# Router product and flip of h2 as one product, with the fourth block's result in the second bank of mix

## The chip, the cores and the metric

The kernel runs on one core of a Trainium2 chip. The metric is the device time in microseconds of one execution; of the kernel before, three runs were timed. One further execution was recorded by the profiler; all rows below come from that one.

## What is computed

A transformer block with adaptive layer norm on x of shape 16 x 512 x 128 (16 batches, 512 tokens, 128 channels), all in fp32:

```
h = layernorm(x) * (1 + ca) + sa
x = x + ga * attention(h)                  # Q = K = V = h @ Wq + bq, one head, softmax
h = layernorm(x) * (1 + cb) + sb           # "h2" in the kernel
route = sigmoid(h @ Wr + br)               # 8 experts
e = argmax(route);  p = max(route)
x = x + gb * p * (gelu(h @ W1[e]) @ W2[e]) # W1 128x512, W2 512x128 per expert
```

sa, ca, ga, sb, cb, gb are rows made from a conditioning input, one per batch. The change touches the line `h @ Wr` and the way in which h2 gets back from its flipped form into rows of tokens.

## The kernel before, in words

**Two phases.** The attention phase handles the 16 batches in slots k = -2 to 15 (`attention_slots`). The second phase handles the expert layer over tiles of up to 256 tokens that are sorted by expert (39 tiles, `ffn_slots`). Between them stand some hand-written steps for batches 14 and 15, whose routing is not done when the last slot ends. Each engine (TensorE `pe`, ScalarE `act`, VectorE `dve`, GpSimd `pool`, the DMA queue `sp`) has its own list of work, written out by hand, and takes it strictly in that order; semaphores join the lists. There is no planner: the functions named `slot(k)` are the order.

**One attention slot k on TensorE** (line 630). Five batches are in the works at once: `before2` (k-2), `before` (k-1), `now` (k), `after` and `after2`. A batch has J = 4 blocks of 128 tokens. The slot's list is: second score product of `now` (score, lines 500 to 502, three fp32r matmuls of 512 columns), flip of the first block's probabilities (L512, four transposes), fourth mix of `before` (L525, eight matmuls), projection of `after` (L479), third score product of `now`, **router of `before2`** (L545), flip of the second block's probabilities, first mix of `now`, fourth score product of `now`, flip of v (L487), **flip of h2 of `before2`** (L555), flip of the third block's probabilities, second mix of `now`, first score product of `after`, fourth flip, places of `before2` (L569 to L575), third mix, and two flips of normalised rows (L469, and L537 for h2 of `before`). In the last slot (k = 15) the first tiles of the second phase are woven in (flip_rows, L587; up, L608 to L610).

**One attention slot on VectorE** (line 1158): maximum of the second scores (`find_max`, L937), third residual of `before` (`residual`, L956) with its statistics (L963), statistics of x for `after2`, maximum of the third scores of `now`, **fourth residual of `before`**, **bias addition of `before2`** (`add_bias`, L989), statistics, split of q (L919), maximum of the fourth scores, choice of the expert of `before2` in six small steps (L1004 to L1021) between other work, first maximum of `after`, slot numbers of `before2` (L1032 to L1044). In slots 13 and 14 chains of tiny instructions that plan the first tiles (`early_plan`) come on top, and in slot 15 VectorE fills the first tile's weights (`fill_slots(0)`, L1073 and L1078) ahead of the maximum of the third scores.

**ScalarE** does the exponentials (L747), the copies of flipped probabilities (L755), scale and shift of h2 into `h2_t` (`router_input`, L763), the exponential for the router (`logit_exp`, L778), the copy of the flipped-back h2 into the payload rows (`ffn_input`, L771) and in the second phase the gelu (L804).

**The path of h2 before the change.** `flip_xn2` puts the normalised rows, flipped, into PSUM bank `side[0]`; ScalarE makes `h2_t` from it (128 channels on partitions, 4 x 128 tokens). `router` multiplies each 128x128 block of `h2_t` (the stationary operand) with Wr (128 x 8, the moving operand) into 4 x 8 columns of `side[0]`. VectorE adds the bias from there. Only when it has read them (`logit_ready`) does `flip_h2` flip the same four blocks back into rows of tokens, over all 512 columns of `side[0]`; `ffn_input` copies them into the payload, and `places` waits for that copy (`h2_ready`) before it uses `side[0]` again. `mix(b, j)` writes the first 128 columns of bank `mixed[j % 2]`, and `residual(b, j)` reads them; the second phase's `down(t)` writes the first 256 columns of `mixed[t % 2]` and `finish(t)` (L1098) reads them.

**The hand-written steps between the phases.** TensorE: fourth mix of batch 15, router(14), down(0), flip_h2(14), up(1), places(14), flip_rows(2), down(1) (L625), flip_xn2(15), up(2), router(15), flip_rows(3), down(2), flip_h2(15), up(3), places(15), and so on. ScalarE: logit_exp(14), ffn_input(14), gelu(1) and so on, where an exponential and a gelu each need their own table, loaded by an instruction of its own.

## Time and profile before

| | |
|---|---|
| median of three runs | 354.69 us (354.61 to 355.04) |
| the profiled execution's own time | 354.34 us |
| span of its profile | 352.6 us |
| TensorE busy | 325.0 us, 92% of the span |
| VectorE busy | 278.9 us, 79% |
| ScalarE busy | 223.5 us, 63% |
| GpSimd busy | 193.1 us, 55% |
| mean granted clock of TensorE | 0.986 of 2.4 GHz |

The span runs from the first to the last instruction of the profile; the execution's own time has 1.74 us around it. PE is TensorE's matmul, PEld its weight load, which overlaps with matmuls; DVE is VectorE, ACT ScalarE, POOL GpSimd. Instructions of one engine overlap by some 0.06 to 0.1 us at their ends, so that the pace of a sequence is read from start to start, not from durations. An fp32 matmul is issued as two weight loads and two matmuls; a transpose as one of each.

### The profile page before, as it was taken

The numbers are of one execution on the slowest core, as the hardware profiler recorded it, in microseconds if no ns is written. First come the engines' busy times: TensorE is split into PE (matmuls) and PEld (weight loads), VectorE is DVE, ScalarE is ACT, GpSimd is POOL, SyncE is SP. The second block draws the span as 40 slices with busy tenths as digits, with TensorE's granted clock in tenths as the row PEclk, the third lists the DMA queues.
The fourth block names the chain that finished last, engine by engine and source line by source line (L and its number), as shares of the span: only waits on it lengthen the run. The fifth ranks groups of instructions, "written<-read, shape, count | busy, mean of one in ns | idle before, by whom it ended". The sixth has DMA issues, their size and how long they took to land.

```text
span 352.6 us, 8419 instructions
## 1 busy us (share of the span) xinstructions
PE 325.0 (92%) x2578; PEld 299.6 (85%) x2578; DVE 278.9 (79%) x1114; ACT 223.5 (63%) x477; POOL 193.1 (55%) x224
## 2 busy tenths in 40 slices
PE   2799999999999999999989898899999999999960
PEld 2388788889888988898878798899999999999960
DVE  5378898898889888988997896899897777877730
ACT  2589987888788878887866585654445454434320
POOL 5016467545754575457525445877566556565661
PEclk9999999999999999999999999999999999999995
DMA  3394124337653666943536612664989554454300
GB/s 113 116 256 104 44 68 131 100 112 121 146 105 104 123 128 188 249 138 111 105 91 224 231 50 87 186 205 134 289 259 307 166 171 120 127 139 125 93 21 4
DMA packets 34493, 49.27 MB, mean 140 GB/s; under 512 B 4320, under 2 KB 26115, under 8 KB 34448
## 3 DMA queue, kind: packets, MB, share of 16 engines
q1 hardware_dynamic: 27504, 31.74, 37.0%
q0 software_dynamic: 6368, 16.92, 12.9%
q8 instruction: 21, 0.34, 0.4%
q14 instruction: 24, 0.20, 0.2%
q10 hardware_dynamic: 576, 0.07, 0.1%
HBM read 28.21 MB, written 20.96 MB: 139 GB/s over the span
## 4 chain that ended last, share of the span: by engine, by line
PE 70%; DVE 13%; ACT 6%; issue 5%; DVEq 2%; DMA 1%; POOL 1%; POOLq 0%; SPq 0%; ACTq 0%
PE mixed L625 14%; PE mixed L525 12%; PE flipped L512 6%; PE side L479 4%; PE scores L502 3%; PE scores L500 3%; PE scores L501 3%; PE side L545 3%; PE side L469 2%; PE scores L609 2%; PE scores L610 2%; PE scores L608 2%; PE side L537 2%; PE side L487 2%; PE flipped L609 2%
## 5 line engine op out<-in xcount | busy, mean ns | idle before, releaser
L1406 POOL DMA_INDIRECT sorted_rows<-payload,slots x64 | 63.9, 998 | 79.8 <-DVE slots L1044 64.9
L1433 POOL DMA_INDIRECT out_dram<-y_out,tokens x71 | 74.9, 1055 | 42.4 <-DVE y_out L1105 25.8
L625 PE MATMUL mixed<-down_slot,hidden 128*128 128x128 f32 x568 | 70.1, 276 | 2.5 <-ACT hidden L804 2.5
L625 PEld LDWEIGHTS mixed<-down_slot,hidden 128*128 128x128 f32 x568 | 66.5, 192 | 3.0 <-ACT hidden L804 3.0
L525 PE MATMUL mixed<-v_sb,probs_t 128*128 128x128 f32 x512 | 69.0, 278 | 0.0
L747 ACT ACTIVATE probs<-scores,row_max 128x512 f32<-128x512 f32 x64 | 44.0, 687 | 35.1 <-DVE row_max L937 33.4
L525 PEld LDWEIGHTS mixed<-v_sb,probs_t 128*128 128x128 f32 x512 | 62.2, 192 | 0.2
L937 DVE TENSOR_REDUCE row_max<-scores 128x1 f32<-128x512 f32 x64 | 44.1, 688 | 19.0 <-PE scores L502 19.0
L789 ACT ACTIVATE f_hi<-side 128x256 fp32r<-128x256 f32 (+1 forms) x39 | 14.3, 366 | 42.8 <-PE side L587 42.8
L512 PE MATMUL flipped<-ident,probs 128*128 128x128 f32 x256 | 39.1, 275 | 0.4 <-ACT probs L747 0.3
L755 ACT ACTIVATE probs_t<-flipped 128x512 f32<-128x512 f32 x64 | 37.9, 594 | 0.0
L512 PEld LDWEIGHTS flipped<-ident,probs 128*128 128x128 f32 x256 | 31.1, 145 | 5.9 <-ACT probs L747 1.9
L500 PE MATMUL scores<-q_hi,q_lo 128*128 128x512 f32 x64 | 35.7, 557 | 0.0
L1073 DVE CAST up_slot<-w_parts 128x1024 fp32r x39 | 28.0, 719 | 3.2 <-issue 1.4
L708 ACT ACTIVATE xn<-x_tile,offset,rstd 128x128 f32<-128x128 f32 x64 | 26.2, 491 | 5.2 <-POOL offset L1379 5.2
L1376 POOL TENSOR_TENSOR rstd<-var,neg_half 128x4 f32<-128x4 f32 x16 | 19.9, 1243 | 15.7 <-DVE var L875 15.4
L804 ACT ACTIVATE hidden<-flipped 128x512 f32<-128x512 f32 x38 | 22.5, 597 | 7.9 <-PE flipped L610 6.0
L1078 DVE COPY down_slot<-w_sb 128x512 f32 x39 | 17.5, 448 | 11.4 <-PE mixed L625 11.4
L502 PE MATMUL scores<-q_hi 128*128 128x512 f32 x64 | 25.5, 398 | 0.0
L501 PE MATMUL scores<-q_lo,q_hi 128*128 128x512 f32 x64 | 25.3, 396 | 0.0
L1098 DVE SCALAR_TENSOR_TENSOR gated<-mixed,rows 128x128 f32<-128x128 f32 x71 | 21.6, 341 | 3.0 <-PE mixed L625 3.0
L608 PE MATMUL scores<-f_lo,up_slot 128*128 128x256 f32 (+1 forms) x80 | 23.5, 294 | 0.0
(187 smaller groups left out, 768.7 us busy)
## 6 DMA issues: line engine op xcount, KB each, us to landing
rows<-sorted_rows SPq DMA_DIRECT2D x32, 388.0 KB, 3.7
x_tile<-in_L_attn_inputs_dram SPq DMA_DIRECT2D x16, 256.0 KB, 3.2
payload<-stored_gates SPq DMA_DIRECT2D x16, 256.0 KB, 9.3
sorted_rows<-pad_rows SPq DMA_DIRECT2D x9, 388.0 KB, 4.6
w_parts<-in_L_ffn_W_dram SPq DMA_DIRECT2D x1, 2048.0 KB, 8.8
rows<-sorted_rows SPq DMA_DIRECT2D x7, 194.0 KB, 2.6
out_dram<-y_out,tokens POOLq DMA_INDIRECT x71
gate<-stored_gates SPq DMA_DIRECT2D x16, 64.0 KB, 5.8
```

Of the source, the lines that this page charges most:

```text
L500: nc.tensor.matmul(o, q_lo[:, b.p, mine], q_hi[:, b.p, :], start=True, stop=False)
L501: nc.tensor.matmul(o, q_hi[:, b.p, mine], q_lo[:, b.p, :], start=False, stop=False)
L502: nc.tensor.matmul(o, q_hi[:, b.p, mine], q_hi[:, b.p, :], start=False, stop=True).then_inc(scores_ready, 1)
L512: last = nc.tensor.transpose(flipped[j % 2][:, k * P:(k + 1) * P], probs[:, j % 2, k * P:(k + 1) * P], ident[:])
L525: last = nc.tensor.matmul(mixed[j % 2][:, 0:H], probs_t[:, j % 2, k * P:(k + 1) * P], v_sb[:, b.p, k, :], start=(k == 0), stop=(k == J - 1))
L608: nc.tensor.matmul(o, hi, f_lo[:, t % 2, 0:width], start=True, stop=False)
L625: last = nc.tensor.matmul(mixed[t % 2][:, u * H:(u + 1) * H], hidden[:, t % 2, f, u * P:(u + 1) * P], down_slot[:, t % 3, f, :], start=(f ...
L747: nc.scalar.activation(probs[:, j % 2, :], scores[j % 2][:], ACT.Exp, bias=row_max[:, c:c + 1], accum_out=den[:, c:c + 1]).then_inc(exp_do ...
L755: nc.scalar.activation(probs_t[:, j % 2, :], flipped[j % 2][:], ACT.Copy).then_inc(probs_t_ready, 1)
L937: nc.vector.tensor_reduce(row_max[:, c:c + 1], scores[j % 2][:], AX_X, ALU.max, negate=True).then_inc(max_found, 1)
L1406: nc.gpsimd.indirect_dma_start(rows_dram, bass.IndirectOffsetOnAxis(ap=slots[:, c:c + 1], axis=0), payload[:, b.q, j, :], None).then_inc(s ...
L1433: nc.gpsimd.indirect_dma_start(out_rows, bass.IndirectOffsetOnAxis(ap=tokens[:, t % RING, u:u + 1], axis=0), y_out[:, t % RING, u, :], Non ...
```

## The change

- `ident` and `wr_sb` become two parts of one buffer `ident_wr` of 128 + 8 columns.
- `router` now multiplies each block of `h2_t` with this 136-column moving operand: the first 128 columns of the result are the block flipped back, the last 8 the logits. Blocks 0 to 2 lie in `side[0]` at a step of 136 columns; block 3, for which that bank has no room, in columns 256 to 391 of `mixed[1]`. `flip_h2` is gone.
- Before the fourth product TensorE waits until the fourth residual of the batch before has been read out of `mixed[1]` (`x1_ready`), and for the last batch until tile 1 of the second phase has (`gated_ready`).
- Before the second mix of a slot, which writes `mixed[1]`, TensorE waits for the bias addition and for ScalarE's copy of block 3.
- ScalarE copies block 3 with an instruction of its own (`ffn_input_part`, right behind `logit_exp`), and blocks 0 to 2 where it copied all four.
- VectorE adds the bias in two instructions, block 3 first. Between the phases `finish(1)` moves ahead of `add_bias(15)`.

```diff
-        ident = sb("ident", [P, P])
+        ident_wr = sb("ident_wr", [P, P + E])
+        ident = ident_wr[:, 0:P]
...
-        wr_sb = sb("wr_sb", [P, E])
+        wr_sb = ident_wr[:, P:P + E]
...
+        def h2_bank(j):
+            if j == J - 1:
+                return mixed[1][:, 2 * H:3 * H + E]
+            return side[0][:, j * (H + E):(j + 1) * (H + E)]
...
                 wait(pe, x1_ready, J * b.n + j - 1)
+                if j == 1:
+                    wait(pe, logit_ready, b.n - 1)
+                    wait(pe, h2_part_ready, b.n - 1)
                 for k in range(J):
                     last = nc.tensor.matmul(mixed[j % 2][:, 0:H], probs_t[:, j % 2, k * P:(k + 1) * P],
...
                 pe.wait_ge(h2t_ready, b.n + 1)
                 for j in range(J):
-                    last = nc.tensor.matmul(side[0][:, j * E:(j + 1) * E], h2_t[:, j * P:(j + 1) * P],
-                                            wr_sb[:], start=True, stop=True)
-                last.then_inc(logits_ready, 1)
-
-            def flip_h2(b):
-                if not real(b):
-                    return
-
-                pe.wait_ge(logit_ready, b.n + 1)
-                for j in range(J):
-                    last = nc.tensor.transpose(side[0][:, j * P:(j + 1) * P], h2_t[:, j * P:(j + 1) * P],
-                                               ident[:])
-                last.then_inc(h2_flipped, 1)
+                    if j == J - 1:
+                        pe.wait_ge(x1_ready, min(J * (b.n + 2), J * B))
+                        if b.n == B - 1:
+                            pe.wait_ge(gated_ready, 4)
+                    last = nc.tensor.matmul(h2_bank(j), h2_t[:, j * P:(j + 1) * P], ident_wr[:],
+                                            start=True, stop=True)
+                last.then_inc(h2_routed, 1)
...
                 flip_v(after)
-                flip_h2(before2)
                 if ending:
...
             down(0)
-            flip_h2(last_but_one)
             up(1)
...
             down(2)
-            flip_h2(last_one)
             up(3)
...
                 act.wait_ge(xn2_flipped, b.n + 1)
-                wait(act, h2_flipped, b.n)
+                wait(act, h2_routed, b.n)
...
+            def ffn_input_part(b):
+                if not real(b):
+                    return
+                act.wait_ge(logit_ready, b.n + 1)
+                wait(act, scattered[b.q], 16 * J * b.r)
+                nc.scalar.activation(payload[:, b.q, J - 1, 0:H], h2_bank(J - 1)[:, 0:H], ACT.Copy
+                                     ).then_inc(h2_part_ready, 1)
+
             def ffn_input(b):
                 if not real(b):
                     return
-                act.wait_ge(h2_flipped, b.n + 1)
-                wait(act, scattered[b.q], 16 * J * b.r)
-                nc.scalar.activation(payload[:, b.q, :, 0:H], side[0][:].rearrange("p (j h) -> p j h", j=J),
-                                     ACT.Copy).then_inc(h2_ready, 1)
+                nc.scalar.activation(payload[:, b.q, 0:J - 1, 0:H], side[0][:, 0:(J - 1) * (H + E)].rearrange(
+                    "p (j h) -> p j h", j=J - 1)[:, :, 0:H], ACT.Copy).then_inc(h2_ready, 1)
...
                 logit_exp(before2)
+                ffn_input_part(before2)
...
-                dve.wait_ge(logits_ready, b.n + 1)
-                nc.vector.tensor_tensor(logit[:].rearrange("p (j e) -> p j e", e=E),
-                                        side[0][:, 0:J * E].rearrange("p (j e) -> p j e", e=E),
-                                        br_sb[:].unsqueeze(1).to_broadcast([P, J, E]), ALU.add
+                dve.wait_ge(h2_routed, b.n + 1)
+                nc.vector.tensor_tensor(logit[:, (J - 1) * E:J * E], h2_bank(J - 1)[:, H:H + E], br_sb[:], ALU.add)
+                nc.vector.tensor_tensor(logit[:, 0:(J - 1) * E].rearrange("p (j e) -> p j e", e=E),
+                                        side[0][:, 0:(J - 1) * (H + E)].rearrange("p (j h) -> p j h", j=J - 1)[:, :, H:H + E],
+                                        br_sb[:].unsqueeze(1).to_broadcast([P, J - 1, E]), ALU.add
                                         ).then_inc(logit_ready, 1)
...
             fill_slots(3)
+            finish(1)
             add_bias(last_one)
-            finish(1)
             split_lo(3)
```

## Rows read from the trace of the kernel before

**Rows 1.** The page: busy us (share of the span), instructions, of all engines.

```profile
PE 325.0 (92%) x2578; PEld 299.6 (85%) x2578; DVE 278.9 (79%) x1114; ACT 223.5 (63%) x477; POOL 193.1 (55%) x224
```

**Rows 2.** Three windows: PE, PEld, DVE, ACT, POOL busy, TensorE's clock, DMA share, GB/s.

```profile
0.00:20.00 20.00, 11.10 (x38) 7.25 (x39) 9.63 (x42) 8.32 (x17) 4.86 (x21) 1.00 0.45 146
100.00:140.00 40.00, 40.00 (x308) 35.95 (x307) 35.40 (x165) 33.20 (x76) 23.33 (x28) 1.00 0.57 132
180.00:220.00 40.00, 36.15 (x295) 32.90 (x295) 31.90 (x141) 26.84 (x55) 18.19 (x20) 1.00 0.39 133
```

**Rows 3.** Timeline of TensorE in one ordinary slot: start, duration (us), line, matmuls.

```profile
161.44 0.39 PE L502 MATMUL scores<-q_hi 128*128 128x512 f32 x1
161.67 0.95 PE L545 MATMUL side<-wr_sb,h_t 128*128 128x8 f32 x8
162.48 0.63 PE L512 MATMUL flipped<-ident,probs 128*128 128x128 f32 x4
162.95 1.06 PE L525 MATMUL mixed<-v_sb,probs_t 128*128 128x128 f32 x8
163.76 0.47 PE L500 MATMUL scores<-q_hi,q_lo 128*128 128x512 f32 x1
...
164.97 0.60 PE L555 MATMUL side<-ident,h_t 128*128 128x128 f32 x4
165.40 0.60 PE L512 MATMUL flipped<-ident,probs 128*128 128x128 f32 x4
```

**Rows 4.** Timeline of VectorE in the same slot; in brackets idle time, releaser.

```profile
161.87 0.69 DVE L937 TENSOR_REDUCE row_max<-scores 128x1 f32<-128x512 f32 x1 [0.28 <-PE scores L502]
162.48 0.34 DVE L956 SCALAR_TENSOR_TENSOR payload<-mixed,den_inv,x_tile 128x128 f32<-128x128 f32 x1
162.74 0.18 DVE L989 TENSOR_TENSOR logit<-side,br_sb 128x32 f32<-128x32 f32 x1
162.86 0.29 DVE L963 BATCH_NORM_STATS2 stats<-payload 128x6 f32<-128x128 f32 x1
...
164.73 0.69 DVE L937 TENSOR_REDUCE row_max<-scores 128x1 f32<-128x512 f32 x1 [0.57 <-PE scores L502]
```

**Rows 5.** Timeline of ScalarE in the same slot: the fourth exponential.

```profile
165.46 0.69 ACT L747 ACTIVATE probs<-scores,row_max 128x512 f32<-128x512 f32 x1 [1.47 <-DVE row_max L937]
```

**Rows 6.** Waits of TensorE, whole span: us in total, times, longest.

```profile
PE side L537 <- DVE batch_count L1035: 2.0, 2, 1.4
```

**Rows 7.** Timeline, last slot and after it: where TensorE starts behind a wait.

```profile
202.14 0.17 DVE L989 TENSOR_TENSOR logit<-side,br_sb 128x32 f32<-128x32 f32 x1
...
202.37 0.66 PE L555 MATMUL side<-ident,h_t 128*128 128x128 f32 x4
...
209.23 1.06 PE L545 MATMUL side<-wr_sb,h_t 128*128 128x8 f32 x8
...
210.15 2.03 PE L625 MATMUL mixed<-down_slot,hidden 128*128 128x128 f32 x16
```

**Rows 8.** Timeline behind the attention phase, ScalarE and TensorE.

```profile
212.65 0.60 ACT L771 ACTIVATE payload<-side 128x512 f32<-128x512 f32 x1 [1.87 <-PE side L555]
...
213.27 1.28 ACT L804 ACT_TABLE_LOAD   x1
...
215.70 2.05 PE L625 MATMUL mixed<-down_slot,hidden 128*128 128x128 f32 x16 [1.26 <-ACT hidden L804]
```

**Rows 9.** Timeline of the last slot, TensorE and VectorE.

```profile
200.09 0.63 PE L512 MATMUL flipped<-ident,probs 128*128 128x128 f32 x4
...
201.88 0.34 DVE L956 SCALAR_TENSOR_TENSOR payload<-mixed,den_inv,x_tile 128x128 f32<-128x128 f32 x1
201.91 0.40 PE L502 MATMUL scores<-q_hi 128*128 128x512 f32 x1
...
202.88 0.68 DVE L937 TENSOR_REDUCE row_max<-scores 128x1 f32<-128x512 f32 x1
```

More of the change, by code:

```diff
@@ L260, in adaln_block @@
         h2t_ready = sem("h2t_ready")
-        logits_ready = sem("logits_ready")
+        h2_routed = sem("h2_routed")
         logit_ready = sem("logit_ready")
@@ L271, in adaln_block @@
         ids_ready = sem("ids_ready")
-        h2_flipped = sem("h2_flipped")
+        h2_part_ready = sem("h2_part_ready")
         h2_ready = sem("h2_ready")
@@ L844, in _ @@
             logit_exp(last_but_one)
+            ffn_input_part(last_but_one)
             ffn_input(last_but_one)
@@ L851, in _ @@
             logit_exp(last_one)
+            ffn_input_part(last_one)
             ffn_input(last_one)
```

## The prediction

> **What bounds the kernel now.** I read the page first: TensorE is busy 92% of the span, VectorE 79% [rows 1]. That is a mean over stages, so next came the windows. In the middle of the attention phase TensorE is busy for all of its 40 us while VectorE and ScalarE have room; in the last slots of that phase it stands idle for 3.85 us of 40 [rows 2]. Then the timeline of one slot, engine by engine. On TensorE groups follow each other without a gap [rows 3], so in such a slot every nanosecond that TensorE issues less is a nanosecond won, and every wait that is put into its queue is a nanosecond lost. VectorE waits for the third score product before its row maximum, 0.28 us, and again 0.57 us before the next one [rows 4]; ScalarE stands idle 1.47 us before the fourth exponential [rows 5]. The last view is the list of waits: where TensorE waits longest inside the attention phase, it is in two slots for VectorE [rows 6].
>
> **What is removed.** The flip of h2, four transposes. From its start to the next group's start is 165.40 - 164.97 = 0.43 us [rows 3]. It goes once per batch, 16 times: 6.9 us if TensorE is what counts everywhere.
>
> **What the wider product costs.** The router's four fp32 products are issued as eight weight loads and eight matmuls. With 8 moving columns they take 162.48 - 161.67 = 0.81 us; the eight matmuls of a mix, with 128 moving columns, take 163.76 - 162.95 = 0.81 us too [rows 3]. So 8 or 128 columns cost the same 0.10 us per matmul and 136 will cost at most 136/128 of that, 0.107 us: 0.05 us for all eight. The Trainium skill (TensorE: Matmul & The Clock Gate, section "Wait — 56ns, not 53.3ns?") puts a matmul of very few columns at a floor near 25 ns and a wide one at N/2.4 + 2.5 ns, which is 59 ns at 136; by that the widening would be an estimated 0.03 us for each matmul and 0.27 us per batch, and most of the saving would go; the rows show equal times at 8 and 128 columns, so the measurement decides.
>
> **What is added: the wait before the fourth product.** The fourth result lies in the second bank of mix, so TensorE waits there until VectorE has made the fourth residual of the batch before, which reads that bank. In VectorE's queue that residual stands behind the row maximum of the third score product, and that product is the group that TensorE has just finished. So the wait is a round trip that starts when TensorE arrives:
> - scores end at 161.44 + 0.39 = 161.83 [rows 3], row maximum starts 161.87, residual starts 162.48 and ends 162.82 [rows 4];
> - a wait of TensorE on VectorE ends 0.06 us after the releasing instruction (VectorE 202.14 + 0.17 = 202.31, TensorE 202.37) [rows 7]: 162.88;
> - the first three products need 6 x 0.10 = 0.61 us from 161.67 and are through at 162.28, so TensorE stands 0.60 us;
> - a start from standstill is dearer: the router's eight pairs that start right behind a wait take 210.15 - 209.23 = 0.92 us [rows 7], against 0.81. I take 0.11;
> - the fourth product's two pairs: 0.21 us.
> The next group starts at 163.20, not 162.48: +0.72. With the flip gone (-0.43) the slot is **longer by 0.29 us**. Bounds: without the dearer start and at 0.10 us a pair, +0.17; if instead the full weight load ahead of the first matmul and a later signal are paid, +0.40.
>
> The Trainium skill (PSUM — Partial Sum Buffer, section "PSUM bank collisions raise a hardware error") says that two engines may not touch one bank at once even at different columns, and to guard by bank: by that rule this wait can't be left out though the columns are disjoint. No run here shows a collision; it changes no number above.
>
> **What queues behind.** TensorE: flip and mix of the next probabilities, the fourth score product, all later by 0.72, by 0.29 after the place of the old flip. VectorE: the bias addition waits for the fourth product, which ends about 0.42 us after its start (1.06 us for eight less six of 0.107 [rows 7]), at 163.30; two small additions take about 0.12 us each, as the one does from 162.74 to 162.86 [rows 4]. What follows is late by about 0.7 us, but the next row maximum had 0.57 us of idle time in front of it and its product comes 0.72 later, so this stays covered. If the cover fails, each slot pays up to 0.1 more. ScalarE's extra copy costs at most the whole copy's 0.60 [rows 8] and lies in the 1.47 us of [rows 5]. TensorE's other new wait, before the second mix, asks for that copy. The additions are through near 163.6; one copy of probabilities, one small exponential and this copy, at most 1.4 us together, bring it to 165.0, and the flip ahead of that mix starts only at 165.40 + 0.29 = 165.69 [rows 3]: nothing. No DMA is added or moved; scatters on GpSimd wait for slot numbers, which shift with everything else.
>
> **The sum, slot by slot.** The router product runs in 14 attention slots.
> - 11 ordinary ones: 11 x 0.29 = +3.2.
> - Two slots in which VectorE is the bound, since it also makes the early plan; TensorE waits there for VectorE, up to 1.4 us [rows 6]. The removed flip brings nothing, and the round trip holds VectorE at its bias addition: +0.72 each, +1.4.
> - The last slot. VectorE first fills the expert weights, so the residual starts at 201.88 and ends 202.22 [rows 9]. TensorE's fourth product can start at 202.28, the next group at 202.60, not 200.09: +2.5. The fourth score product starts 201.91 + 2.51 = 204.42 and ends 204.82; its row maximum, which ran at 202.88 [rows 9], starts at 204.86: **+1.98**. The exponentials, the last flip, the choice of expert and the first up product hang on it one after another.
> - Behind the attention phase: ScalarE's copy no longer waits for the flip (1.87 us idle before it), so the table load behind it and the gelu of tile 1 come earlier, and with them the down product that waited 1.26 us [rows 8]. But VectorE's chain, over the normalised rows that GpSimd's power gives, then decides, which leaves 0.5; the wait of the last batch's fourth product for tile 1's gating takes that back; the same at tile 3 leaves about 0.2. I take **-0.2**; bounds -1.4 (the whole wait) and +0.5.
> Sum: 3.2 + 1.4 + 2.0 - 0.2 = +6.4 us.
>
> The profiled execution took 354.34 us (span 352.6 and 1.74 around it); the median of the runs is 354.69, 0.35 above it. On the median: 354.69 + 6.4 = **361.1 us**.
>
> **Rivals.**
> 1. The wait doesn't hold TensorE: the residual is there when TensorE reaches the fourth product. Then only the saving counts: 16 x (0.43 - 0.05) = -6.1 us, 348.6. It decides from the point at which the residual ends before 162.28, and in the rows it ends 0.54 later in every ordinary slot, because the row maximum in front of it waits for TensorE itself. Chance 0.05.
> 2. A draw: TensorE starts again without loss (+0.17 for 11 slots, 1.9), the last slot's and the plan slots' delays are taken up by the idle time around them (up to 3 of 3.4), and the down product gains its whole 1.26. Sum near +1, 355.6; each part would have to fall the kind way. Chance 0.07 for anything from here to 357.
> 3. VectorE's cover fails: held by the fourth product, it comes late to its maximum in every slot, the fourth exponential and flip follow. Price: the 0.40 bound and 0.1 more for 14 slots, +3 on the sum, 364. For it speaks that 0.57 is less than 0.7; against it that the product is late by the same 0.72. Chance 0.13.
> 4. The standstill of some 2.4 us in the last slot lowers TensorE's granted clock. In the first 20 us TensorE is busy for 11 us only and the clock stays at 1.00, 2.4 GHz [rows 2], so I hold it unlikely; it would cost what the next few us of work lose at the lower level, 1 to 2 us, inside the range. Chance 0.03.
> My own case has the remaining 0.72.
>
> **How the numbers follow.** The bounds: 11 x 0.17 + 2 x 0.5 + 1.0 - 1.4 = +2.5, and 11 x 0.40 + 2 x 0.9 + 2.3 + 0.5 = +9.0. Both ends need every term at its bound at once, so I cut the low one only a little (+2.8, 357.5) and the high one nowhere near rival 3's 364 (364.0). Within 0.2% (0.7 us, about what a measurement of this kernel can tell from no change) lies a corner of rival 2: 0.02. Faster: rival 1 and the far end of rival 2: 0.06. Slower: 0.92.
>
> **What would show it.** Right: in ordinary slots TensorE stands 0.6 us inside the router line, waiting for the residual line; the distance from one batch's router line to the next grows by about 0.3 us; the bias additions wait for the router line; the last slot shows a stand of over 2 us. The eight wide matmuls of the batch after the attention phase take 0.9 to 1.0 us. Wrong: no idle time on TensorE before the fourth product (rival 1); row maxima of the fourth product without any idle time before them (rival 3); a distance between router lines that shrinks by 0.4 us.

## The result, and the profile after

| | before | after |
|---|---|---|
| median (six runs each) | 354.87 us (354.59 to 355.69) | 364.68 us (363.48 to 365.65) |
| the profiled execution's own time | 354.34 us | 364.71 us |
| span | 352.6 us | 363.0 us |

The change makes the kernel slower: ratio 1.0273, 95% interval 1.0256 to 1.0290. The forecast was 361.1 us with a range to 364.0: the direction was right, the size was 3.6 us short, and the result lies outside the range.

The page of the kernel after, busy us (share of the span) and instructions, against [rows 1]:

```profile
PE 328.7 (91%) x2514; PEld 296.7 (82%) x2514; DVE 281.2 (77%) x1130; ACT 226.2 (62%) x493; POOL 190.5 (52%) x224
```

TensorE has 64 instructions fewer (the flips) and 3.7 us more busy time. Where the 10.4 us of span came from shows in the distances from one batch's router line to the next, batch by batch (start of L545 before, of L558 after, read from the timelines):

| stretch | before | after | difference |
|---|---|---|---|
| start to the first router line | 43.28 | 43.39 | +0.11 |
| first distance | 12.60 | 12.66 | +0.06 |
| ten ordinary slots, together | 117.56 | 123.54 | +5.98 (0.60 each) |
| the two slots of the early plan | 13.51, 12.33 | 14.16, 12.99 | +0.65, +0.66 |
| the last slot | 9.95 | 12.98 | +3.03 |
| between the phases | 10.22 | 9.88 | -0.34 |
| router line of batch 15 to the end | 133.15 | 133.40 | +0.25 |

The sum is +10.4. The ten ordinary distances are 11.75 to 11.77 before; after, eight are 12.31 to 12.36, one is 12.39 and one 12.47. So a slot of the steady kind costs 0.58. The first distance hardly grows, although the wait is there too: in it TensorE waits for VectorE's `mask` in both kernels, 0.28 us before and 0.17 after, and both times reaches the line behind that wait about 6.75 us after the router line.

Timeline of TensorE in one ordinary slot of the kernel after (the one of [rows 3], now 5.53 us later):

```profile
166.97 0.39 PE L508 MATMUL scores<-q_hi 128*128 128x512 f32 x1
167.20 0.86 PE L558 MATMUL side<-ident_wr,h_t 128*128 128x136 f32 x6
168.40 0.50 PE L558 MATMUL mixed<-ident_wr,h_t 128*128 128x136 f32 x2 [0.35 <-DVE payload L965]
168.74 0.60 PE L518 MATMUL flipped<-ident_wr,probs 128*128 128x128 f32 x4
...
170.53 0.39 PE L508 MATMUL scores<-q_hi 128*128 128x512 f32 x1
```

VectorE in that slot, against [rows 4], in the same view:

```profile
167.40 0.69 DVE L946 TENSOR_REDUCE row_max<-scores 128x1 f32<-128x512 f32 x1 [0.27 <-PE scores L508]
168.00 0.34 DVE L965 SCALAR_TENSOR_TENSOR payload<-mixed,den_inv,x_tile 128x128 f32<-128x128 f32 x1
168.94 0.17 DVE L998 TENSOR_TENSOR logit<-mixed,br_sb 128x8 f32<-128x8 f32 x1 [0.59 <-PE mixed L558]
...
170.96 0.69 DVE L946 TENSOR_REDUCE row_max<-scores 128x1 f32<-128x512 f32 x1 [0.56 <-PE scores L508]
```

ScalarE, against [rows 5]:

```profile
171.69 0.69 ACT L747 ACTIVATE probs<-scores,row_max 128x512 f32<-128x512 f32 x1 [1.43 <-DVE row_max L946]
```

The router line to the next line is 168.74 - 167.20 = 1.54 us, against 0.81: +0.73. It is the round trip that was forecast: TensorE stands behind its six matmuls until the residual is through (168.00 + 0.34 = 168.34, start 168.40). The idle time in front of the fourth maximum is as before, 0.56 us. So up to here the slot went as forecast. The list of waits of TensorE over the whole span, against [rows 6]:

```profile
PE mixed L558 <- DVE payload L965: 7.1, 14, 2.2
```

Fourteen waits for the residual, one per attention slot with a router line. (The view counts idle time from the modelled end of the sixth matmul; the six take 0.69 from start to start, as in the kernel with the residual first below, so the stand is 168.40 - 167.89 = 0.51.)

What the forecast didn't have shows only at the end of the slot. TensorE, ScalarE and VectorE there, in three cuts of the timeline of the kernel after:

```profile
161.49 1.14 PE L534 MATMUL mixed<-v_sb,probs_t 128*128 128x128 f32 x8
162.58 0.66 PE L475 MATMUL side<-ident_wr,xn 128*128 128x128 f32 x4
163.17 0.63 PE L546 MATMUL side<-ident_wr,xn 128*128 128x128 f32 x4
163.55 0.47 PE L506 MATMUL scores<-q_hi,q_lo 128*128 128x512 f32 x1
```

```profile
160.88 1.64 ACT L708 ACTIVATE xn<-x_tile,offset,rstd 128x128 f32<-128x128 f32 x4
```

```profile
158.63 0.69 DVE L946 TENSOR_REDUCE row_max<-scores 128x1 f32<-128x512 f32 x1 [0.55 <-PE scores L508]
...
162.83 0.19 DVE L1042 TENSOR_TENSOR place<-side,region 128x32 f32<-128x32 f32 x1
```

The same lines of the kernel before, in an ordinary slot:

```profile
132.74 1.14 PE L525 MATMUL mixed<-v_sb,probs_t 128*128 128x128 f32 x8
133.72 0.60 PE L469 MATMUL side<-ident,xn 128*128 128x128 f32 x4
134.15 0.60 PE L537 MATMUL side<-ident,xn 128*128 128x128 f32 x4
134.51 0.48 PE L500 MATMUL scores<-q_hi,q_lo 128*128 128x512 f32 x1
```

```profile
129.47 0.69 DVE L937 TENSOR_REDUCE row_max<-scores 128x1 f32<-128x512 f32 x1 [0.57 <-PE scores L502]
...
133.70 0.18 DVE L1032 TENSOR_TENSOR place<-side,region 128x32 f32<-128x32 f32 x1
```

After the change the flip of the normalised rows (L475) starts 0.06 us behind the end of ScalarE's four normalisations (162.52), and the flip behind it (L546) 0.15 us behind the end of VectorE's `place` (163.02), whose source bank it overwrites. Before, `place` ended at 133.88 and the flip came 0.27 later, in TensorE's own time. From the third mix to the first score product the kernel after takes 2.06 us, the one before 1.77 (134.51 - 132.74): 0.29 of the flip's 0.43 are lost here.

That makes the slot a **loop of two engines**: TensorE from that flip to the end of the fourth score product, then VectorE from the fourth row maximum to `place`, then the flip again. After: 163.17 to 170.92 is 7.75, the hand-over 0.04, VectorE's list 158.63 to 163.02 is 4.39, the hand-over back 0.15; sum 12.33, which is the distance measured. Before: 7.03 (L537 at 157.66, L502 ending at 164.69), 0.04 and 4.41; with the hand-over back of the kernel after, 0.15, they make 11.63, while TensorE's own list makes 11.75. The loop lay only 0.12 us under TensorE's list, though no wait showed it. The flip of h2 lies outside the loop (it comes behind the fourth score product), the new wait lies inside.

The last slot in the kernel after, TensorE's timeline, against [rows 9]:

```profile
206.74 0.86 PE L558 MATMUL side<-ident_wr,h_t 128*128 128x136 f32 x6
209.76 0.50 PE L558 MATMUL mixed<-ident_wr,h_t 128*128 128x136 f32 x2 [2.16 <-DVE payload L965]
210.10 0.60 PE L518 MATMUL flipped<-ident_wr,probs 128*128 128x128 f32 x4
...
212.23 0.63 PE L507 MATMUL scores<-q_lo,q_hi 128*128 128x512 f32 x1
212.66 0.63 PE L508 MATMUL scores<-q_hi 128*128 128x512 f32 x1
```

and the windows of that stretch (PE, PEld, DVE, ACT, POOL busy, TensorE's clock, DMA share, GB/s), against [rows 2]:

```profile
210.00:211.00 1.00, 1.00 (x11) 1.00 (x11) 0.64 (x4) 0.26 (x1) 0.00 (x0) 1.00 0.53 199
211.00:212.00 1.00, 1.00 (x7) 1.00 (x6) 0.17 (x1) 0.62 (x3) 0.73 (x1) 0.51 0.00 0
...
214.00:215.00 1.00, 1.00 (x9) 1.00 (x8) 1.00 (x9) 0.95 (x3) 0.00 (x0) 0.79 0.00 0
```

TensorE stands for 2.3 us (six products through at 206.74 + 0.69 = 207.43, next start 209.76), and from about 211 to 214.4 its clock is granted at 0.50, 1.2 GHz. From the flip at 210.10 to the third score matmul at 212.66 are 2.56 us; the same steps take 170.53 - 168.74 = 1.79 in the ordinary slot: 0.77 lost to the clock. That matmul itself then takes 0.63 instead of 0.39, another 0.24.

### The profile page after: what moved, and what is told of

It is laid out like the page before. It is cut to its first block and busy times, and to the rows that moved or that the text cites. A ratio compares the mean times of both kernels' runs of the same rounds, so it can differ in the third digit from the quotient of the medians.

```text
span 363.0 us, 8338 instructions
## 1 busy us (share of the span) xinstructions
PE 328.7 (91%) x2514; PEld 296.7 (82%) x2514; DVE 281.2 (77%) x1130; ACT 226.2 (62%) x493; POOL 190.5 (52%) x224
## 5 line engine op out<-in xcount | busy, mean ns | idle before, releaser
L518 PE MATMUL flipped<-ident_wr,probs 128*128 128x128 f32 x256 | 39.2, 276 | 0.4 <-ACT probs L747 0.3
L518 PEld LDWEIGHTS flipped<-ident_wr,probs 128*128 128x128 f32 x256 | 31.7, 143 | 5.6 <-ACT probs L747 1.5
L1083 DVE CAST up_slot<-w_parts 128x1024 fp32r x39 | 27.2, 698 | 3.0 <-issue 1.4
L1088 DVE COPY down_slot<-w_sb 128x512 f32 x39 | 19.2, 493 | 13.0 <-PE mixed L628 13.0
L1386 POOL TENSOR_TENSOR rstd<-var,neg_half 128x4 f32<-128x4 f32 x16 | 17.7, 1105 | 16.1 <-DVE var L884 15.8
```

The costliest lines, as they stand in the source:

```text
L518: last = nc.tensor.transpose(flipped[j % 2][:, k * P:(k + 1) * P], probs[:, j % 2, k * P:(k + 1) * P], ident[:])
L1083: nc.vector.tensor_copy(up_slot[:, t % 2, :, :].rearrange("p s f -> p (s f)"), w1_parts[:].rearrange("p e s f -> p (e s f)")[:, bass.ds(w ...
```

## The experiments

In the expectations "theory P" is the prediction's reckoning, in which the removed flip counts in full, "theory L" is the loop above, and "theory C" an earlier form of it. On two chips the kernel before itself has a median of 370 to 374 us, and in most ordinary slots of the traces taken there ScalarE stands still before a copy, for up to 1.5 us, without a cause in the trace ("disturbed" below). Every ratio is against the runs of before on the same chip. A slot without such a stand isn't a clean measure there either: in the kernel without the flip it has 11.78 and 11.81 us, against 11.64 for the same slot on a quiet chip.

**The wait alone.** The kernel before, with the wait and nothing else; the flip stays.

```diff
                 for j in range(J):
+                    if j == J - 1:
+                        pe.wait_ge(x1_ready, min(J * (b.n + 2), J * B))
                     last = nc.tensor.matmul(side[0][:, j * E:(j + 1) * E], h2_t[:, j * P:(j + 1) * P],
```

> The kernel before with one thing added: TensorE waits before the fourth router product (still 8 columns, still in the first side bank) until the fourth residual of the batch before is made. The flip of h2 stays. Theory C (the wait costs 0.73 us in every slot; the flip that is removed in the changed kernel brings back only about 0.14 of its 0.43 us, since behind the fourth score product the lists of VectorE and ScalarE are only some 0.2 us shorter than TensorE's; and the stand of over 2 us in the last slot drops TensorE's clock to 1.2 GHz for about 3 us, 1.0 us more): distance between router lines 12.47 us, 11 x 0.72 + 2 x 0.7 + 2.0 + 1.0 = +12.3, about 367 us, with a window of clock 0.5 behind the last slot's wait. Theory P (the prediction's sum: the flip is worth its whole 0.43 and the clock stays): the same distance 12.47, no lower clock, +11.3, 366. Both fall if the distance stays near 11.75 to 12.0.

Measured: 381.34 us against 373.22 there, ratio 1.0213 (1.0138 to 1.0288). All ten ordinary distances are 12.40 to 12.42 (although ScalarE stands still there too): the wait alone costs a slot 0.65 us, more than the whole change (0.58). The wait carries the loss, and all the rest of the change brings 0.07. In the last slot TensorE stands until 210.25, and its granted clock is 0.50 from 211.6 to 215.0, as theory C had it. The total grew by 8.1 us and not by the 11 or 12 of either theory; on this chip that can't be taken apart.

**The flip alone.** The kernel before without the flip of h2; its result, the rows of h2 in the payload, is then missing.

```diff
-                pe.wait_ge(logit_ready, b.n + 1)
-                for j in range(J):
-                    last = nc.tensor.transpose(side[0][:, j * P:(j + 1) * P], h2_t[:, j * P:(j + 1) * P],
-                                               ident[:])
-                last.then_inc(h2_flipped, 1)
+                return
...
-                wait(act, h2_flipped, b.n)
+                wait(act, logits_ready, b.n)
...
-                act.wait_ge(h2_flipped, b.n + 1)
+                act.wait_ge(logit_ready, b.n + 1)
```

> The kernel before without the four transposes of h2; everything else stays, the router with 8 columns and no new wait. It leaves out the flip back of h2, so the rows of h2 that go to the experts hold other numbers; routing is the same. Theory P: every ordinary slot is 0.43 us shorter, distance 11.32, and about 0.3 from the copy behind the attention phase: 354.7 - 4.7 - 0.3 = 349.7 us. Theory C: TensorE waits at the end of each slot instead, for the normalised x of ScalarE and for VectorE's slot numbers; distance 11.6 to 11.65, 353 us.

> The same kernel as in the run without the flip of h2 (the four transposes are left out, the rows of h2 for the experts hold other numbers), on another call, since ScalarE and VectorE stood for up to 1.5 us in many slots of that run for nothing in the kernel. Theory L (the ordinary slot is a loop of two engines: TensorE from the last flip of a slot to the fourth score product, 7.0 us, then VectorE's list from that product's row maximum to the slot numbers, 4.4 us, together 11.5 with their signals, against 11.75 of TensorE's own work; so 0.43 us less TensorE work can't bring more than 0.2): distance 11.55 to 11.65, 352.5 to 353.5 us if the kernel before takes 354.7. Theory P (the flip counts in full): 11.32, 349.7 us.

> The kernel before without the flip of h2 a third time (the four transposes left out, other numbers in the rows of h2), since the first two were on a chip on which the kernel before takes 373 to 374 us. Theory L (a loop of TensorE and VectorE's list behind the fourth score product, 11.5 us long with its signals): distance between router lines 11.55 to 11.65 and 352.5 to 353.5 us where the kernel before takes 354.7. Theory P (TensorE's work is the bound and the flip counts in full): 11.32 and 349.7 us. Theory S (ScalarE's 1.4 us stands before the copy of the second flipped probabilities belong to the other chip): none of them here; if they are here too they belong to the kernel.

Measured: 0.9962 (0.9917 to 1.0007) and 0.9839 (0.9681 to 0.9997) on a disturbed chip, which doesn't settle a few tenths per cent; on a chip with 354.67 for before it is 353.11, ratio 0.9950 (0.9932 to 0.9969), 1.6 us. Nine of the ten distances are 11.61 to 11.67 and one is 11.73, mean 11.66: leaving out 0.43 us of TensorE's work shortens the slot by 0.10, as theory L had it (11.55 to 11.65); theory P had 11.32. The end of the slot in that kernel, TensorE and VectorE:

```profile
167.53 1.14 PE L525 MATMUL mixed<-v_sb,probs_t 128*128 128x128 f32 x8
168.69 0.66 PE L469 MATMUL side<-ident,xn 128*128 128x128 f32 x4
169.24 0.63 PE L537 MATMUL side<-ident,xn 128*128 128x128 f32 x4
169.63 0.47 PE L500 MATMUL scores<-q_hi,q_lo 128*128 128x512 f32 x1
```

```profile
168.93 0.17 DVE L1028 TENSOR_TENSOR place<-side,region 128x32 f32<-128x32 f32 x1
```

Mix to score product takes 2.10 us (1.77 before), and the flip starts 0.14 behind the end of `place`, as in the kernel after. The 0.12 of the loop's slack is what can be had, and 0.10 was.

**One bank.** All four wide products in `side[0]`, the fourth first; block 3 overlaps block 2 by 32 columns, so its result is partly overwritten. No wait, no second bank.

```diff
-                return mixed[1][:, 2 * H:3 * H + E]
+                return side[0][:, 512 - H - E:512]
...
-                if j == 1:
-                    wait(pe, logit_ready, b.n - 1)
-                    wait(pe, h2_part_ready, b.n - 1)
...
-                for j in range(J):
-                    if j == J - 1:
-                        pe.wait_ge(x1_ready, min(J * (b.n + 2), J * B))
-                        if b.n == B - 1:
-                            pe.wait_ge(gated_ready, 4)
+                for j in (J - 1, 0, 1, 2):
```

> The changed kernel with all four wide products in the first side bank, the fourth computed first and 32 of its columns overwritten by the third (so that 32 of 128 columns of h2 are wrong in every fourth block; routing is right); the wait for the residual and both waits before the second mix are gone, everything else as changed. It takes away the second bank and nothing else. Theory P: no stand in the router, distance 11.37, 354.7 - 11 x 0.38 - 0.2 = 350.3 us. Theory C: distance 11.6, waits of 0.2 to 0.3 us in all before the two flips at the slot's end as in the changed kernel, clock 1.00 in the last slot, 352.5 to 353.5 us. Both: the second bank costs over 10 us.

> The same kernel as in the run with all four wide products in the first side bank (32 of 128 columns of h2 wrong in every fourth block), repeated for the same reason. Theory L: distance 11.60 to 11.65, 353 us; theory P: 11.37, 350.3 us.

Measured: ratio 0.9928 (0.9878 to 0.9978), then 0.9867 (0.9665 to 1.0069), distance in the one slot of each trace that has no stand of ScalarE 11.83 and 11.82, in most others 11.80 to 11.95. Against the 12.33 of the kernel after the loss is gone, and the 11.37 of theory P doesn't show. Whether a saving of a tenth or two is in it this chip can't tell, since the kernel without the flip has 11.78 and 11.81 in that slot here. The ratios below 1 aren't explained by these slots.

**The residual first.** The kernel after with one line moved on VectorE: the fourth residual goes ahead of the maximum of the third scores, so that it no longer stands behind the product that TensorE has just made.

```diff
+                residual(before, 3)
                 if planning:
                     early_plan(0)
...
                 find_max(now, 2)
...
-                residual(before, 3)
```

> The changed kernel with VectorE's fourth residual of the batch before moved ahead of the row maximum of the third scores (in slots 13 and 15 also ahead of the plan and of the filling of weights). The result stays right. If the wait is the round trip over the row maximum, the stand in the router disappears (0.00 instead of 0.35 to 0.60 us) and with it the one of 2.2 us in the last slot and the lower clock. Theory P: distance 11.37, 350.5 us. Theory C: distance 11.6, 353 us, a little under the kernel before. A rival to both: the row maximum comes 0.1 to 0.3 later because the residual lies in front of it and the exponentials follow, distance 11.7 to 11.9, 355 us.

> The same kernel as in the run with the fourth residual ahead of the row maximum, repeated for the same reason. Theory L: no stand in the router, distance 11.60 to 11.65, 353 us; theory P: 11.37, 350.5 us.

> The changed kernel with the fourth residual ahead of the third row maximum, again. Theory L: no stand in the router, distance 11.60 to 11.65, 352.5 to 353.5 us, a little faster than the kernel before. Theory P: 11.37, 350.5 us. If the changed kernel's loss were not the wait: over 360 us.

Measured: 0.9858 (0.9741 to 0.9975) and 0.9934 (0.9891 to 0.9977) on the disturbed chip; on a chip with 354.67 for before 354.92, ratio 1.0008 (0.9995 to 1.0021). TensorE's timeline in a slot of the last of these:

```profile
162.81 0.86 PE L558 MATMUL side<-ident_wr,h_t 128*128 128x136 f32 x6
163.50 0.40 PE L558 MATMUL mixed<-ident_wr,h_t 128*128 128x136 f32 x2
163.73 0.60 PE L518 MATMUL flipped<-ident_wr,probs 128*128 128x128 f32 x4
```

The residual (162.63 + 0.34 = 162.97) is through before the fourth product needs it. The router line takes 0.92 us, the clock in the last slot stays at 1.00, and eight of the ten distances are 11.74 to 11.78, the others 11.81 and 11.86. Theory L had 11.60 to 11.65 here and missed: its loop has the router line with 8 columns. TensorE's part of it runs from the flip to the end of the fourth score product, and the router line lies inside:

```profile
158.75 0.63 PE L546 MATMUL side<-ident_wr,xn 128*128 128x128 f32 x4
...
165.53 0.39 PE L508 MATMUL scores<-q_hi 128*128 128x512 f32 x1
```

That is 7.17 us, against 7.03 before; with 0.04, 4.41 and 0.15 the loop is 11.77, which is the distance measured. The 0.11 of the wider product uses up the 0.12 that the removed flip could have brought.

One moved line gives back all 9.8 us: the wait with what hangs on it is the whole loss, and what is left of the change, flip removed and product widened, is worth nothing as the kernel stands.

**What the loop holds back.** To the kernel with the residual first, a second move: the choice's first two steps ahead of the fourth row maximum, which shortens VectorE's list inside the loop.

```diff
-                find_max(now, 3)
                 choose(before2, 0)
                 invert_den(now, 0)
                 choose(before2, 1)
+                find_max(now, 3)
                 residual(now, 0)
```

> The changed kernel with the fourth residual first and, besides, three small VectorE instructions (the first two of the choice of expert and the reciprocal of the sums) moved from behind the fourth row maximum to ahead of it, into idle time. The result stays right. Theory L: VectorE's list behind the fourth score product is 0.3 us shorter, so the loop is 11.3 and TensorE's own work of 11.37 counts: distance 11.35 to 11.45, 11 x 0.35 plus the parts of the later slots, about 349.5 us, faster than both kernels. Theory P: the three moves change nothing against the run with the residual first, since TensorE is the bound there already. A rival: the exponential of the logits is not ready when VectorE gets to them, VectorE waits in front of the fourth row maximum and the distance grows to 11.7 or more.

> As before this, with the first two steps of the choice and the reciprocal also ahead of the fourth row maximum, again. Theory L: VectorE's list behind the fourth score product 0.3 us shorter, distance 11.35 to 11.45, about 350 us. On the other chip VectorE waited 0.86 us for the exponential of the logits and the distance was 12.4; if that belongs to the kernel, it is 12.4 here too and 361 us.

Measured: on the disturbed chip 1.0121 (0.9963 to 1.0279), nine of the ten distances 12.40 to 12.57. VectorE waits there for the router's exponential nine times, 7.8 us in all; in the other chip's trace that wait is absent from the ordinary slots. On the disturbed chip ScalarE stands 1.2 us and more before the copy ahead of that exponential. On the other chip 353.89, ratio 0.9976 (0.9965 to 0.9987), distance 11.60: the only version that is right and faster than both kernels, by 0.8 us, but far from the 11.35 to 11.45 that I had expected. The cut of its timeline says why (ScalarE, then TensorE):

```profile
164.61 0.69 ACT L747 ACTIVATE probs<-scores,row_max 128x512 f32<-128x512 f32 x1 [1.41 <-DVE row_max L946]
...
165.29 0.48 ACT L777 ACTIVATE payload<-side 128x384 f32<-128x384 f32 x1
165.66 0.60 ACT L755 ACTIVATE probs_t<-flipped 128x512 f32<-128x512 f32 x1
166.14 1.64 ACT L708 ACTIVATE xn<-x_tile,offset,rstd 128x128 f32<-128x128 f32 x4
```

```profile
166.72 1.14 PE L534 MATMUL mixed<-v_sb,probs_t 128*128 128x128 f32 x8
167.83 0.66 PE L475 MATMUL side<-ident_wr,xn 128*128 128x128 f32 x4
168.33 0.60 PE L546 MATMUL side<-ident_wr,xn 128*128 128x128 f32 x4
```

The normalisations end at 167.78 and the flip starts at 167.83, 1.11 behind the mix instead of 0.98. VectorE's `place` ended at 168.00, 0.33 before L546 starts, and no longer holds it. Behind VectorE's loop lies a second one over ScalarE: fourth exponential, two copies, four normalisations. Its parts are TensorE from L546 to the end of the fourth score product (156.72 to 163.84) 7.12, row maximum 0.04 later, exponential 0.73 after that, 3.17 to the end of the normalisations, 0.05, and 0.50 from L475 to L546: 11.61, and the distance measured is 11.60.

**The moves without the change.** Are the 0.8 us those of the change or of the moves? The kernel before, with both moves.

> The kernel before (flip of h2 kept, no second bank, no wait) with VectorE's two moves: the fourth residual ahead of the maximum of the third scores, and the choice's first steps ahead of the maximum of the fourth. Against h3 (the same moves on the kernel after: 353.89 us, ratio 0.9976, distance 11.60) this leaves exactly the change itself. Theory L (the slot is a loop of TensorE and VectorE, and TensorE's own work of 11.75 us is 0.2 longer than it in the kernel before): with the flip kept TensorE's own work bounds, the distance between router lines stays 11.75 and the time 354.5 to 354.9 us, ratio 0.999 to 1.001; the change is then worth some 0.8 us once its wait is gone. Rival A: the moves alone shorten the slot (distance 11.60, time 353.9) and the change itself adds nothing. Rival B: with the old order of TensorE the moved choice makes VectorE late for the fourth exponential: distance over 11.85, time over 356.

> The kernel of i1 once more, hoping for a chip that takes some 354.7 us for the kernel before (the chip of i1 takes 365 to 375, with stands of ScalarE that the profiled run of before doesn't have). Theory L: TensorE's own work bounds while the flip is kept, distance 11.75, ratio 0.999 to 1.001; the 0.8 us that h3 has over the kernel before then belongs to the change. Rival A: the moves alone shorten the slot, distance 11.60, ratio 0.998. Rival B: VectorE's moved steps make the fourth exponential late, distance over 11.85, ratio over 1.003.

Measured: first on a chip with 370.38 (365.2 to 375.15) for before: ratio 1.0251 (1.0155 to 1.0347), with ScalarE's stands in most slots and one slot without them, of 11.76; that tells nothing. Then on a chip with 354.85: 355.33, ratio 1.0020 (1.0010 to 1.0031), all ten ordinary distances at 11.75 or 11.76. With the flip kept, TensorE's own list bounds at 11.75, whatever VectorE does earlier. The 0.5 us that the total is above before lie elsewhere: the first distance is 12.85 instead of 12.60 and the last slot's 10.47 instead of 9.95, while the two plan slots are 0.31 shorter together. So both moves without the change bring a slot nothing, the change with the first move alone brings nothing, and the change with both moves 0.15 us a slot.

**Both kernels again, and the clock.** Before and after unchanged, as anchors, and the kernel after with ten repeats of the third product, in the last slot only, in front of the wait: TensorE works while it would stand.

```diff
                     if j == J - 1:
+                        if b.n == B - 3:
+                            for _ in range(10):
+                                nc.tensor.matmul(h2_bank(2), h2_t[:, 2 * P:3 * P], ident_wr[:],
+                                                 start=True, stop=True)
                         pe.wait_ge(x1_ready, min(J * (b.n + 2), J * B))
```

> The kernel before, unchanged, to see where the chip of the runs so far (373 to 374 us) loses time against the one of the first traces (354.7). Theory S: the stands of ScalarE of 1.4 us before the copy of the second flipped probabilities belong to that chip: they are there in this kernel too, the distance between router lines is 11.8 to 12, and most of the 18 us lie behind the attention phase. Theory K: they belong to the kernels without the flip or without the router's wait: they are absent here and the distance is 11.75.

> The changed kernel, unchanged, on the same chip: distance 12.33 in the ordinary slots as in its first trace if the loop through the wait sets it, whatever the chip does elsewhere; 14 waits for the fourth residual; slower than the kernel before by 2 to 3% on this chip too. If the wait hides what this chip loses elsewhere, under 2%.

> The changed kernel with the third wide product repeated ten times in the last attention slot, in the time in which TensorE stands for the fourth residual (2.2 us in the changed kernel's first trace, in which the clock then was 0.50 for 3.4 us). The result stays right, and TensorE's queue holds 20 more matmuls, 2.1 us, all of them inside the wait. If the stand is what drops the clock, the clock stays 1.00 behind it and the kernel is 1.0 to 1.3 us faster than the changed kernel. If the clock drops for another reason, the time is the same or up to 0.2 us longer and the 0.50 remains.

Measured: before 354.75 against 354.69 (1.0003); after 364.34, ratio 1.0268 (1.0251 to 1.0285), nine ordinary distances 12.31 to 12.39 and one 12.44. With the repeats 364.31, ratio 1.0277 (1.0260 to 1.0294). The windows of the last slot, first of the kernel after in this second trace, then with the repeats:

```profile
210.00:211.00 1.00, 1.00 (x5) 1.00 (x6) 0.26 (x3) 0.06 (x1) 0.00 (x0) 0.50 0.53 199
```

```profile
211.00:212.00 1.00, 1.00 (x12) 1.00 (x11) 0.66 (x5) 0.72 (x3) 0.19 (x1) 1.00 0.16 59
212.00:213.00 1.00, 1.00 (x8) 0.82 (x7) 0.12 (x1) 0.17 (x1) 1.00 (x2) 1.00 0.00 0
```

With the stand filled the clock stays at 1.00 and the last slot's distance is 11.84 us, against 12.98 and 13.44 in the two traces of after. In all three the fourth product starts 3.02 us after the router line, so the repeats delay nothing, and the difference comes behind it. So the stand lowers the clock, and that costs 1.1 to 1.6 us of the last slot.

In the profiled executions this reaches the end: from the last slot's router line to the end of the span are 155.2 us with the repeats, 156.3 and 157.0 without. In the medians, 0.03 apart, the 1.0 to 1.3 us that I had expected don't show. Part of the trace with the repeats' gain is lost at its start, where its first router line comes 0.5 us later (43.93 against 43.39 and 43.44). There the clock matters too: TensorE's first score products run at the lower level in every trace, and the clock record starts, at full clock, between 18.4 and 21.2 us. In the twelve traces in which that is before 20.0 us the first router line comes at 43.15 to 43.55, in the six in which it is after 20.4 (that with the repeats is one, at 20.5) at 43.70 to 44.31. Of the ten executions of the kernel after, the two with the highest mean clock (0.990 and 0.991) took 364.65 and 364.08 us, in the midst of the others. How much of the clock's cost an ordinary execution pays in its total is therefore open.

## Where the prediction was right, and where it failed

- **The added wait** was right in place, cause and size: forecast +0.72 to the start of the next group, measured +0.73. Of its parts, six products 0.69 (0.61), the stand 0.51 (0.60), the last two pairs with their restart 0.34 (0.32). Rival 1 is out; the wait holds in all 14 slots.
- **The wider product** was small, as forecast: eight wide matmuls without a wait take 163.73 - 162.81 = 0.92 us in the kernel with the residual first, against 0.81 with 8 columns. I had 0.05 for the eight and it is 0.11. The Trainium skill's floor for small matmuls (TensorE: Matmul & The Clock Gate, "Wait — 56ns, not 53.3ns?") gave an estimate of 0.27 for the widening; the measured 0.11 is less than half of it.
- **The step that failed: "With the flip gone (-0.43) the slot is longer by 0.29 us."** I took the saving in full, because on TensorE groups follow each other without a gap [rows 3]. That holds for what is added, as long as it is inside the loop; it doesn't hold for what is removed. The rows showed one engine that is full; a second path, through VectorE's list from the fourth score product to the next flip of normalised rows, was 0.12 us shorter, and a third, through ScalarE's, a little shorter still; no wait view shows a path that is only just hidden. Along the second path the same delay gives 11.63 + 0.72 = 12.35 for the slot, and 12.33 was measured. The flip alone is worth 0.10 (kernel without the flip); of the 0.43 in the change 0.15 came (0.73 - 0.58). Ten slots at 0.60 instead of 0.29, and the first, are 6.0 and not 3.2: 2.8 of the missing 4.0 us of the profile. The last slot has another 1.05.
- **The plan slots** were right, +0.65 and +0.66 for 0.72: for these I had argued that VectorE bounds and the removed flip brings nothing. An argument of the same kind held for every slot.
- **The last slot**: +3.03 for +1.98. The delay to the maximum of the fourth scores, from the router line, is 213.32 - 206.74 = 6.58 against 202.88 - 199.28 = 3.60, 2.98 more. With the stand filled, and the clock at 1.00, that maximum starts at 212.88 behind a router line at 207.29: 5.59, 1.99 more. So the round trip of the last slot was reckoned right, and the 0.99 above it is the clock (1.60 in the second trace of after). The maximum with the stand filled:

```profile
212.88 0.69 DVE L950 TENSOR_REDUCE row_max<-scores 128x1 f32<-128x512 f32 x1 [1.15 <-PE scores L508]
```

- **The clock** was my rival 4, priced at 1 to 2 us, and held unlikely (0.03), because TensorE had been busy for only 11 of the first 20 us and [rows 2] give 1.00 for them. That reading was wrong. The record of the clock starts at 18.4 us in that trace, and the view counts what lies before it as full clock; the score products of the kernel before tell the level:

```profile
16.53 0.63 PE L501 MATMUL scores<-q_lo,q_hi 128*128 128x512 f32 x1
16.96 0.63 PE L502 MATMUL scores<-q_hi 128*128 128x512 f32 x1
...
18.55 0.39 PE L501 MATMUL scores<-q_lo,q_hi 128*128 128x512 f32 x1
18.77 0.40 PE L502 MATMUL scores<-q_hi 128*128 128x512 f32 x1
```

The first two follow each other at 0.43 us and take 0.63, as those of 212.23 and 212.66 do at a granted clock of 0.50; the later two at 0.22 to 0.23. So TensorE ran at the lower of its two levels, 1.2 GHz, through its first 18 us with their gaps, and the row was no evidence against the rival (the mean clock of 0.986 in the table of before has the same gap). Rival 4 was true, together with my own case.

- **Behind the attention phase** -0.34 and +0.25 for -0.2: right within 0.1.
- **Rival 3** gave a time close to the result, 364, by luck, since its mechanism was another one: VectorE late at the row maximum. The maximum kept its 0.56 us of idle time; what came late was the end of VectorE's list. What I had written, "in ordinary slots the distance grows by about 0.3 us", is where the trace says wrong.

Open: why on some chips ScalarE stands still before copies and the kernel before takes 370 to 374 us; and what part of the clock's 1.1 to 1.6 us reaches the end of an ordinary execution.

## What to carry to other kernels

An engine without gaps tells what an added nanosecond costs, not what a removed one brings: before a saving is counted, follow the loop through the other engines (their lists from what this engine gives them to what it needs back) and compare its length with the engine's own list; the saving ends at the difference, here 0.12 of 0.43 us, and what the change adds inside the loop comes off it. Ahead of a wait that is put into a full engine's queue, look at what stands in front of the releasing instruction on its own engine: moving one line of VectorE took the whole 9.8 us back. Two edits that bring nothing alone (the change without its wait, VectorE's moves) can bring something together, when each frees one of two bounds that lie close.

## What the runs showed of the hardware

A stand of TensorE of 2.3 us in the middle of dense work was followed by a stretch at a granted clock of 0.50 (1.2 instead of 2.4 GHz). In the trace shown above the stand ends at 209.76 and the granted clock is 0.50 from about 211.0 to 214.4; in the second trace of the same kernel it ends at 209.89, and the clock is 0.50 from about 209.9 to 213.2; in the kernel with the wait alone it ends at 210.25, and the clock is 0.50 from 211.6 to 215.0. So with the same stand the clock fell once at its end and twice 1.2 to 1.4 us later, when TensorE was working again. Work that filled the stand kept it at 1.00, and the stands of 0.51 us in every other slot never lowered it. At the start of every trace, with TensorE idle for much of the time, it ran at the lower level, until 18.4 us in the kernel before, although [rows 2] say 1.00.

An engine's list that starts behind a wait costs more than the wait: the four transposes of L475 take 0.50 from start to start behind ScalarE's release (168.33 - 167.83, in the kernel with both moves), against 0.43 to 0.44 in the flow, and the router's last two pairs 0.34 against 0.23 in the kernel with the residual first.
